# Two semaphores for finished dense evictions, and another wait first, in a two-layer conditioned transformer on Trainium2

## What is computed

```python
mod = silu(condition) @ Wada + bada            # 6 vectors per sequence
xm = layernorm(x) * (1 + sc_a) + sh_a
x = x + gt_a * causal_attention(xm)            # softmax(q k^T / 4, causal) v, then Wproj
xm = layernorm(x) * (1 + sc_m) + sh_m
x = x + gt_m * (gelu(xm @ W1 + b1) @ W2 + b2)
# second layer
h = sln(x)                                     # gamma * layernorm + beta, from the condition
h1 = full_attention(h) @ Wp.T + bp + x         # softmax(q k^T) / 16
out = sln(h1) + h1
```

## Time and profile before

| what | value |
|---|---|
| median of 3 runs | 1254.23 us (1252.0 to 1255.34) |
| profiled execution, its span | 1249.3 us |
| instructions in the span | 18813 |
| PE busy | 1168.6 us (94%) |
| DVE busy | 850.9 us (68%) |
| ACT busy | 678.2 us (54%) |
| POOL busy | 279.0 us (22%) |
| chain that ended last | PE 59%, DVE 20%, ACT 6%, SPq 5%, DMA 5%, issue 3% |

### The profile page before, as it was taken

How to read it: one execution, slowest core, us unless ns; L and a number is a source line. 1 busy time by engine, 2 the same in 40 slices (tenths; PEclk the granted TensorE clock), 3 DMA queues, 4 the chain that set the end, 5 groups by cost and what they waited for, 6 DMA issues and landing times.

```text
span 1249.3 us, 18813 instructions
## 1 busy us (share of the span) xinstructions
PE 1168.6 (94%) x6604; PEld 591.7 (47%) x6604; DVE 850.9 (68%) x1779; ACT 678.2 (54%) x1346; POOL 279.0 (22%) x378
## 2 busy tenths in 40 slices
PE   7888989999899998999899999999989999999995
PEld 4434644464444644555344644446445553445332
DVE  4735498637886579836887378855788368754775
ACT  1272145656557465565555565564655656543673
POOL 1133022311332023311233013320243002310003
PEclk9898999999999999999999999999999999989998
DMA  5603031301432032500524024310425005200311
GB/s 177 192 2 102 2 112 41 111 12 65 117 87 69 19 109 74 135 4 19 149 52 118 2 73 109 100 57 18 113 69 137 1 2 162 39 17 25 91 33 42
DMA packets 59191, 89.36 MB, mean 72 GB/s; under 512 B 12914, under 2 KB 23762, under 8 KB 59098
## 3 DMA queue, kind: packets, MB, share of 16 engines
q1 hardware_dynamic: 58078, 87.35, 24.9%
q10 hardware_dynamic: 1020, 0.81, 0.2%
HBM read 24.41 MB, written 4.70 MB: 23 GB/s over the span
## 4 chain that ended last, share of the span: by engine, by line
PE 59%; DVE 20%; ACT 6%; SPq 5%; DMA 5%; issue 3%; POOL 1%; ACTq 0%; DVEq 0%; POOLq 0%
PE X L1034 13%; DVE MX L760 10%; PE OP L942 10%; PE X L1083 9%; PE X L1059 9%; PE SC L953 8%; PE X L972 8%; SPq L412 4%; ACT E L619 3%; DMA OC<-OE 2%; DVE STAT L769 2%; DMA QS<-NT 2%; DVE XN L812 1%; DVE XR L878 1%; DVE TMP L874 1%
## 5 line engine op out<-in xcount | busy, mean ns | idle before, releaser
L760 DVE TENSOR_REDUCE MX<-X 128x1 f32<-128x512 f32 (+3 forms) x1024 | 533.4, 581 | 187.6 <-PE X L975 100.0
L619 ACT ACTIVATE E<-SC 128x512 f32<-128x512 f32 (+3 forms) x1024 | 459.8, 525 | 323.6 <-PE SC L953 258.1
L972 PE MATMUL X<-KS,QS 96*128 96x512 bf16 (+3 forms) x1024 | 296.6, 346 | 10.7 <-DVE MX L760 6.4
L953 PE MATMUL SC<-QS,KS 99*128 99x512 bf16 (+3 forms) x1024 | 276.3, 342 | 24.9 <-ACT E L619 15.9
L942 PE MATMUL OP<-E,V 128*32 128x512 f32 (+3 forms) x2048 | 207.6, 523 | 6.2 <-ACT OE L634 5.4
L953 PEld LDWEIGHTS SC<-QS,KS 99*128 99x128 bf16 x1024 | 93.3, 97 | 176.0 <-ACT E L619 112.4
L972 PEld LDWEIGHTS X<-KS,QS 96*128 96x128 bf16 x1024 | 97.5, 98 | 160.5 <-DVE MX L760 51.2
L537 POOL TENSOR_SCALAR_AFFINE_SELECT E<-E 128x512 f32<-128x512 f32 x128 | 86.8, 680 | 252.4 <-ACT E L619 252.4
L1083 PE MATMUL X<-XT,W 128*128 128x512 f32 x256 | 123.8, 618 | 2.1 <-ACT XT L652 2.1
L1059 PE MATMUL X<-XT,WQKV 128*128 128x512 f32 x256 | 117.0, 602 | 1.5 <-ACT XT L652 1.5
L1034 PE MATMUL X<-W,HID 128*128 128x256 f32 x512 | 115.3, 380 | 0.4 <-ACT HID L672 0.4
(11 more groups left out here) (92 smaller groups left out, 920.4 us busy)
## 6 DMA issues: line engine op xcount, KB each, us to landing
QS<-PART SPq DMA_DIRECT2D x192, 128.0 KB, 2.4
KS<-PART SPq DMA_DIRECT2D x192, 128.0 KB, 2.5
OC<-OE SPq DMA_DIRECT2D x56, 128.0 KB, 3.9
RB<-recip_sums SPq DMA_DIRECT2D x56, 128.0 KB, 2.6
XIN<-in_x SPq DMA_DIRECT2D x8, 512.0 KB, 5.0
ROW<-row_vectors SPq DMA_DIRECT2D x8, 512.0 KB, 3.6
out<-OUT SPq DMA_DIRECT2D x7, 512.0 KB, 3.4
W<-in_w SPq DMA_DIRECT2D x2, 1024.0 KB, 6.7
```

The source lines that it names most:

```text
L619: a.activation(E[:, at["tick"].index() % 3, j, lo:T], SC[(at["head"].index() + j) % 3][:, lo:T], ACT.Exp, scale=HD ** -0.5 if layer == 0 e ...
L760: v.reduce_max(MX[:, qt, h:h + 1], X[at["bank"].index() % BANKS][:, 0:w], AX.X, negate=True)\
L953: t_.matmul(SC[(at["head"].index() + j) % 3][:, lo:T], KS[stacks(layer, b)][0:ALL_ROWS, h, kt * P:kt * P + P], QS[stacks(layer, b)][0:ALL_ ...
L972: ins = t_.matmul(bank[:, 0:w], QS[stacks(layer, b)][0:CUT_ROWS, h, qt * P:qt * P + P], KS[stacks(layer, b)][0:CUT_ROWS, h, 0:w], start=Tr ...
```

## The change

dense_done is replaced by two semaphores: dense_act, raised by ScalarE's evictions, and dense_dve, raised by VectorE's. Two new counts, by_act and by_dve, take the place of "dense" in all waits for finished evictions; BY_ACT lists the chunks that ScalarE evicts. Each count is in the order of one engine's queue, so the waits of bank(0) for all earlier evictions are dropped (VectorE keeps one ahead of a fold, which overwrites RG). TensorE waits for dense_act or dense_dve, whichever belongs to the eviction in question; the first product of a step group waits for dense_dve alone.

Secondly, where the code waits for several semaphores ahead of one instruction, their order in the code is altered in many places, so that another one stands first. No compute instruction, DMA or matmul is added, removed or moved.

In the diff's core, shown below, lines of the same kind on other chunks are left out.

```diff
+BY_ACT = ("turn_a", "turn_m", "turn_1", "merge0", "merge1") + tuple(f"up_{_n}" for _n in range(FT))
...
+    if "dense" in _adds:
+        _adds["by_act" if _n in BY_ACT or _n.startswith("max") else "by_dve"] = _adds["dense"]
...
# GpSimd, q0 and k0
+                    wait(pool, dense_dve, at["by_dve"].at(1, 2))
                     wait(pool, cut_low, c.at())
-
-                    wait(pool, dense_done, at["dense"].at(1, 2))
...
# ScalarE, exponentials
+                        wait(act, head_full, at["head"].at(1, j + 1))
                         if j == 0:
-
                             wait(act, pv_done, at["tick"].at(1, -2))
-                        wait(act, head_full, at["head"].at(1, j + 1))
...
# ScalarE, bank(); the same on VectorE
                 def bank(k):
-                    if k == 0:
-
-                        wait(act, dense_done, c.at())
                     wait(act, dense_full, c.at(1, k + 1))
...
# ScalarE, GELU
                     a.activation(HID[:, ht, :], bank(0)[:], ACT.Gelu, bias=B1[:, ht:ht + 1])\
-                        .then_inc(dense_done, 1)
+                        .then_inc(dense_act, 1)
...
# VectorE, q and k
-                    wait(dve, cut_low, at["low"].at())
-                    wait(dve, dense_done, c.at())
                     for t in range(2):
                         wait(dve, high_act, at["high"].at(1, t + 1))
+                        if t == 0:
+                            wait(dve, cut_low, at["low"].at())
...
# VectorE, proj0, down_1, down_3
-                    wait(dve, row0_dma, at["rows0"].at(16))
-                    wait(dve, bias_pool, at["bias"].at())
-                    wait(dve, plus_pool, at["gain"].at())
-                    if what == "down_1":
-                        wait(dve, hold_pool, at["hold"].at())
...
+                        two, psum = slice(2 * tp, 2 * tp + 2), bank(n)
+                        if n == 0:
+                            wait(dve, row0_dma, at["rows0"].at(16))
+                            wait(dve, bias_pool, at["bias"].at())
+                            wait(dve, plus_pool, at["gain"].at())
+                            if what == "down_1":
+                                wait(dve, hold_pool, at["hold"].at())
...
# TensorE, products
-                wait(pe, exp_done, at["step"].at(4, 4 * n + 4))
                 if layer == 0:
                     wait(pe, masked_pool, at["masked"].at(1, n + 1))
+                wait(pe, exp_done, at["step"].at(4, 4 * n + 4))
                 if s == 0:
 
-                    wait(pe, dense_done, at["dense"].at())
+                    wait(pe, dense_dve, at["by_dve"].at())
...
# TensorE, bank()
-                    claim(at["bank"].at(1, k), dense_done, c.at(1, k + 1))
+                    if "by_act" in ADDS[what]:
+                        claim(at["bank"].at(1, k), dense_act, at["by_act"].at(1, k + 1))
+                    else:
+                        claim(at["bank"].at(1, k), dense_dve, at["by_dve"].at(1, k + 1))
...
# TensorE, transposes of XN
+                        if ft == 0:
+                            wait(pe, norm_dve, at["norm"].at(4, -3))
                         psum = bank(ft)
...
# TensorE, transposes of the maxima
+                    wait(pe, max_pool, at["maxima"].at(4, 4))
                     psum = bank(0).bitcast(BF16)
...
-                    wait(pe, max_pool, at["maxima"].at(4, 4))
```

More of the change, by code:

```diff
@@ L130 @@
           "rows1", "x_in", "gain", "close", "stack0", "stack1", "high", "low", "norm", "head", "tick",
-          "step", "masked", "group", "scan", "halves", "fold", "bank")
+          "step", "masked", "group", "scan", "halves", "fold", "bank", "by_act", "by_dve")
 class Count:
@@ L883, in work @@
                 elif what == "proj1":
-                    wait(dve, plus_pool, at["gain"].at())
-                    wait(dve, hold_pool, at["hold"].at())
                     for tp in range(2):
-                        v.tensor_tensor(TMP[:, 2 * tp:2 * tp + 2, :], bank(tp)[:].rearrange("p (t d) -> p t d", d=D),
-                                        RH[:, 2 * tp:2 * tp + 2, :], ALU.add).then_inc(dense_done, 1)
-                    wait(dve, dense_done, c.at(1, 2))
+                        psum = bank(tp)
+                        if tp == 0:
+                            wait(dve, plus_pool, at["gain"].at())
+                            wait(dve, hold_pool, at["hold"].at())
+                        v.tensor_tensor(TMP[:, 2 * tp:2 * tp + 2, :], psum[:].rearrange("p (t d) -> p t d", d=D),
+                                        RH[:, 2 * tp:2 * tp + 2, :], ALU.add).then_inc(dense_dve, 1)
+                    wait(dve, dense_dve, at["by_dve"].at(1, 2))
                     stats(at, TMP)
```

64 lines of the change are left out of this document (32 added, 32 removed).

## The result

The changed kernel takes 1239.22 us (median of 6 runs, 1234.44 to 1242.8) against 1254.01 us for the kernel before (6 runs, 1252.0 to 1258.25): a ratio of 0.9887, 95% interval 0.9862 to 0.9912, or 14 us (14.8 between the medians). Run again later beside others it took 1238.55 us, ratio 0.9879 (0.9851 to 0.9906). The prediction was 1249.2 us with a range from 1244.7 to 1252.8.

A forecast was written before the change was run, and what follows sets the result against it. TensorE held 59% of the chain; only waits could shorten. Terms 1.9 + 1.1 + 1.1 + 0.5 + 2.2 - 0.2 made 6.6 us, credited as 5.0: 1254.2 to 1249.2 us, range 1244.7 to 1252.8.

The forecast's parts named there:

- terms 1 to 4: Last waits moved into the instruction: ScalarE 1.9 us, VectorE 1.1, TensorE 1.1; GpSimd's cast starting earlier 0.5.
- one E, one NT, one TMP, two transposes, one cast in each: Shortened waits counted on the chain in each of the five full passes: 0.47 us a pass, 2.35 us together.
- Term 2: VectorE: seven TMP products, two reciprocals, two scalings of OC and one X32 start sooner; 1.1 us.
- term 4: GpSimd's cast of the low parts starts 0.08 us earlier at six places, beside VectorE's first proj0 addition; 0.5 us.
- Term 5: Waits for the other engine's eviction end: XT near 111 us 1.0, first product after max0 0.75, NT at 1139 0.5; 2.2 us.
- Term 6: Cost where another wait ends last: an E released by a product, a maxima transpose, one of XN; 0.2 us lost.
- Term 7: Earlier ScalarE table loads, own-eviction waits between GELUs and masked_pool's order were held to be worth nothing.
- SyncE's queue is untouched: Remark among the items worth nothing: the change leaves SyncE's queue alone; no time was credited.
- Rival (b), the clock, 0.14: Less TensorE idleness near 112 us removes a half-speed stretch: a further 3.1 us, 1246.1 us, low end 1244.7; chance 0.14.
- 4.9 us lie outside the span.: Difference between the profiled execution's 1249.3 us span and the 1254.23 us median, taken as untouched by the change.
- a little over half: Credit for head and tail terms, 2.8 us, while nearly all was credited in the passes, 2.2 us.

The follow-up runs named there:

- vector_old_order: Changed kernel with VectorE's wait order alone undone (TMP, X and the scaling of OC wait for their bank last again); 1237.93 us, ratio 0.9877.
- filler_before: Kernel before with 6 and 10 transposes of the identity in TensorE's two waits ahead of up_0, first pass only; 1250.75 us, ratio 0.9980.
- xt_waits_filled: Changed kernel with ScalarE's first XT waiting for VectorE's V again in pass 0, and ten transposes filling TensorE's wait; 1239.68 us, ratio 0.9900.
- after_again: The changed kernel, unaltered, timed and profiled again beside the follow-up kernels; 1238.55 us, ratio 0.9879 against the kernel before.
- sums_last_after: Changed kernel with SyncE issuing the row sums RS behind the four compact transfers OC<-OE instead of ahead; 1289.02 us, ratio 1.0298.

## Why the prediction was wrong, point by point

- **Latencies (rows to terms 1 to 4).** Right for each row: 0.02 us for E, TMP and NT, 0.04 for the transposes, 0.08 for an E behind a product, 0.08 for GpSimd's cast. The step that failed is the count: "one E, one NT, one TMP, two transposes, one cast in each", 0.47 us a pass. Aligned row by row, TensorE gains 0.04 to 0.07 us at some ten places of a pass, most of them scores that wait for an E, up to 0.09 at one and 0.14 at the transposes of the maxima near 468 us: 0.78 us a pass without the store (0.45 to 1.0 in single passes). The chain names one releaser at each point. My reading is that another path, near enough to take over, carries the same kind of wait and is not on it, and that the gain counts in full because both became shorter; no run isolates that. I took such near ties as a reason to credit less.
- **Term 2, VectorE: 1.1 us.** Wrong: nothing that can be told (vector_old_order). At the earlier trace rows it counted a place that term 4, GpSimd's cast, had counted already: 0.07 us is gained there once, with TMP's new order or without it.
- **Term 5, no more waiting for the other engine: 2.2 us.** Right in the main. XT gave 0.93 us (predicted 1.0), the first product 0.67 (0.75, aligned at 59.93 us). At 1139 us NT starts 0.5 us earlier as predicted, but only 0.12 of it reaches TensorE. Together 1.7 us.
- **Term 6.** Right in kind; nothing in the traces is later by more.
- **Term 7, the table loads.** They start earlier, as at 113.90 us in after right behind XT, and near 112 us the same step of 3.07 us with the load late (filler_before) and early (xt_waits_filled) says that it is worth nothing there, as predicted. Elsewhere it was not tested.
- **What was missing: the store.** "SyncE's queue is untouched" was true and beside the point. The engine that changed was the one whose transfer runs next to SyncE's: 0.12 us more distance took 1.2 us off a transfer that TensorE waited for, 0.43 to 0.48 us a pass, 2.3 us in all. The five rows of the chain with 3.45 to 3.50 us of DMA QS<-NT, against 2.28 us at 51.24 us, the only other one on it, were there to be asked about.
- **Rival (b), the clock, 0.14.** It happened in after and after_again, with the price that it named (3.1 us), and by the cause that it named: filling the idle time removes the stretch and putting the wait back brings one again. Part of it is luck, since behind the shortened gap three profiles of seven still have a stretch, of 3.4 us. It should have been part of the forecast all the same. The Trainium skill, "TensorE: Matmul & The Clock Gate", "Part 1: The HAM clock gate", has activity release the throttle; the three profiles with filled waits agree, at this place. I read its remark on variation from run to run as a reason to keep the chance low, while six profiles of six with the long gap had the stretch, and behind the shorter one four of seven were free of it.
- **"4.9 us lie outside the span."** Wrong: 1.8 us. The other 3.1 us are the difference between that execution and the median, probably its better start.
- **Crediting "a little over half".** No discount was due: without the store and the clock 9.8 us were found where 6.6 us stood on the list and 5.0 us were credited.

The sum, from the rows of after_again against before: 6.2 us from 345 to 1070 us (five passes; the store 2.3, latencies the other 3.9), 1.7 from the evictions of the other engine, 3.1 of clock at 112.6 us, and 4.2 us that are left over in head and tail, where 2.05 us stood on my list. The 4.2 are a remainder and not a sum of priced terms: over thirty steps of 0.04 to 0.07 us like those of the passes, and a few of 0.2 to 0.4 (at 73.0, 226.4 and 253.1 us) that no run explains. Together 15.2 us, against 14.7 between the medians of that call. The 3.4 us that the start cost in these two profiles are no part of it. Without the clock it is 12.1 us; the fit at equal clock has 10.3 to 11.5 for this kernel and its two equals. The fit gives the clock more: 0.0048 of mean clock, 5 us, of which the traces place 3.1.

## What to carry to other kernels

- Align the two traces row by row, or in a forecast ask of every wait of the bottleneck engine what the second-latest releaser is. If it carries the same kind of wait, the saving can count in full; if it is other work, as GpSimd's cast beside TMP, it does not count.
- When something is made earlier by a tenth of a microsecond, list the transfers on other queues within half a microsecond of its own. A small transfer that someone waits for, issued just ahead of a large one that nobody waits for, is worth a look by itself.
- A wait that leaves the bottleneck engine idle ahead of dense work has two prices, its length and the clock after it. A filler of harmless transposes tells the two apart. See to it that the filler does not change the order of the waits around it.

## What the runs showed of the hardware

- A 24 KB transfer on ScalarE's queue with a 512 KB store issued behind it on SyncE's: 3.03 to 3.21 us at 0.28 us of distance, either 1.85 or 2.9 at 0.33, 1.9 at 0.40, 1.85 at 2.7 us. Beside the transfers OC<-OE it took 2.6 to 3.7 us in before with no store near.
- A wait that an instruction holds itself costs 22 to 24 ns from the raising of the semaphore on ScalarE and VectorE and 0.04 us on TensorE; in a separate instruction 83 ns on ScalarE, 79, 93 and 122 ns on VectorE (122 with two of them), and 0.14 us on TensorE.
- TensorE idle for 2.1 us ahead of the matmuls of up_0: 1.2 GHz for 3.4 or 6.8 us in six profiles of six; for 1.2 us: in three of seven; filled with transposes: in none of three.
- Half-speed stretches in a steady loop come in some passes and not in others, but all fifteen outside sums_last_after began at one place of the pass, behind a group of TensorE's waits of 0.6 to 1.7 us; partly filling one of them did not remove them.
